# An audio tower on one core: row scales in two parts, the first batch normalised and projected between the last two convolution groups, and an earlier place for VectorE's shared-expert outputs

## The reference

```python
h = layernorm(conv(x, kernel 2, stride 2) + bias + pair_mean(x)) * gamma + beta   # 188 rows per batch
n = layernorm(h)
q, k, v = n@W_q, n@W_k, n@W_v
lat = (k + v) @ W_down_kv
o = softmax(q @ (lat@W_up_k).T / sqrt(256) * exp(-0.01*|t-s|)) @ (lat@W_up_v)     # 16 heads of 16
h = h + o @ W_o
n = layernorm(h)
h = h + experts(n) + (gelu(n@Sg.T) * (n@Su.T)) @ Sd.T   # 16 experts; each takes its 752 best tokens
```

## Time and profile before

| what | us |
|---|---|
| median of 3 runs (lowest, highest) | 1759.16 (1757.37, 1760.4) |
| the profiled execution: its time, its span in the trace | 1760.71, 1758.9 |
| TensorE, VectorE busy | 1628.6, 1211.9 |
| GpSimd, ScalarE busy | 1026.2, 933.0 |

### The profile page before, as it was taken

One profiled execution on the slowest core, in us unless ns is written; L12 is line 12 of the kernel. 1 busy time (PEld: TensorE's weight loads), 2 busy tenths in 40 slices (PEclk: granted clock), 3 DMA queues, 4 the chain that ended last, 5 costly groups with the idle time before them and its releaser, 6 DMA issues.

```text
span 1758.9 us, 46442 instructions
## 1 busy us (share of the span) xinstructions
PE 1628.6 (93%) x14944; PEld 1200.7 (68%) x14944; DVE 1211.9 (69%) x3836; ACT 933.0 (53%) x2182; POOL 1026.2 (58%) x1101
## 2 busy tenths in 40 slices
PE   5893899999999997899996899999999999999997
PEld 5882667777777774666664577777777777777775
DVE  3884889999999998757788555555555555555541
ACT  3543777777777775453345444444445544444431
POOL 3782265666666655732255446666776666666665
PEclk9995999999999999899998899999999999999999
DMA  6541455666666662432321323444433333434322
GB/s 187 161 141 36 116 146 134 152 151 153 145 145 150 150 150 78 140 79 69 96 79 58 144 81 89 105 106 106 108 102 102 102 90 98 104 85 104 83 32 29
DMA packets 181154, 192.95 MB, mean 110 GB/s; under 512 B 120776, under 2 KB 153928, under 8 KB 175176
## 3 DMA queue, kind: packets, MB, share of 16 engines
q1 hardware_dynamic: 145992, 141.19, 28.4%
q0 software_dynamic: 35072, 50.62, 14.1%
HBM read 134.59 MB, written 50.44 MB: 105 GB/s over the span
## 4 chain that ended last, share of the span: by engine, by line
PE 51%; DVE 3%; ACT 2%; issue 2%; POOL 1%; DMA 1%; SPq 1%; DVEq 0%; POOLq 0%; ACTq 0%
PE psum L1907 28%; PE psum L1926 14%; PE psum L1756 4%; PE psum L1773 2%; PE psum L1887 1%; DVE arena L1347 1%; PE psum L1817 1%; DVE hidden L1350 1%; POOL arena L461 0%; ACT arena L851 0%; DMA weights_lo<-e_u 0%; DVE arena L1317 0%; ACT arena L1041 0%; PE psum L1746 0%; ACT hidden L851 0%
## 5 line engine op out<-in xcount | busy, mean ns | idle before, releaser
L1907 PE MATMUL psum<-arena,hidden 128*128 128x376 f16 x3072 | 493.9, 323 | 2.4 <-DVE arena L1516 1.5
L1907 PEld LDWEIGHTS psum<-arena,hidden 128*128 128x128 f16 x3072 | 300.8, 98 | 191.4 <-DVE arena L1516 2.7
L743 POOL TENSOR_TENSOR arena<-arena 128x376 f16<-128x376 f32 x256 | 250.8, 982 | 201.3 <-ACT arena L851 199.9
L851 ACT ACTIVATE arena<-arena 128x376 f16<-128x376 f32 (+11 forms) x636 | 288.1, 464 | 63.4 <-DVE arena L1436 53.5
L1094 ACT ACTIVATE arena<-psum 128x376 f32<-128x376 f32 x256 | 123.7, 483 | 342.0 <-PE psum L1907 342.0
L1250 DVE CUSTOM_DVE_ANT_0 arena<-psum,constants 128x188 f32<-128x188 f32 x768 | 237.6, 347 | 53.0 <-PE psum L1584 42.9
L851 ACT ACTIVATE arena<-psum 128x188 f32<-128x188 f32 (+7 forms) x457 | 176.0, 398 | 165.3 <-PE psum L1887 72.2
L1516 DVE SCALAR_TENSOR_TENSOR arena<-psum,arena 128x376 f32<-128x376 f32 x256 | 140.5, 549 | 178.4 <-ACT arena L1094 176.7
L1926 PE MATMUL psum<-hidden,arena 128*128 128x256 f16 (+1 forms) x2304 | 256.6, 272 | 0.0
L1926 PEld LDWEIGHTS psum<-hidden,arena 128*128 128x128 f16 (+1 forms) x2304 | 230.3, 103 | 21.4
L900 ACT ACTIVATE arena<-psum 128x376 f32<-128x376 f32 x384 | 184.2, 481 | 81.1 <-PE psum L1598 80.1
(11 more groups left out here) (168 smaller groups left out, 2783.2 us busy)
## 6 DMA issues: line engine op xcount, KB each, us to landing
arena<-e_d SPq DMA_DIRECT2D x16, 1024.0 KB
arena<-e_g SPq DMA_DIRECT2D x15, 1024.0 KB
arena<-e_u SPq DMA_DIRECT2D x15, 1024.0 KB, 5.0
arena<-x_t SPq DMA_DIRECT2D x32, 376.0 KB, 3.4
weighed<-arena POOLq DMA_DIRECT2D x32, 376.0 KB, 3.7
arena<-q_halves SPq DMA_DIRECT2D x192, 47.0 KB, 3.1
arena<-k_halves SPq DMA_DIRECT2D x96, 94.0 KB, 2.3
arena<-q_halves SPq DMA_DIRECT2D x96, 94.0 KB, 2.2
```

The source lines that it names most:

```text
L743: nc.gpsimd.tensor_tensor(dst, f, hi, ALU.subtract).then_inc(ready, 1)
L851: return nc.scalar.activation(dst, src, ACT.Copy, scale=scale)
L1907: last = mm(bank[2 * (s % 2) + i][:, 0:CHUNK], w_, a, start=n == 0, stop=n == 5)
```

## The change

1. No engine meets between convolution and attention. The row scales come in two parts: tiles 0 to 47 (`NORMALS`) once `of_normal(11)` is done, on VectorE behind `of_conv(14)`; tiles 48 to 63 at the end, on ScalarE behind its body(-3).
2. Batch 0 is normalised, transposed and split between groups 14 and 15 (`before_last`), and its x, Q and K go to banks 0, 1 and 2, which group 14 has left. The buffers XN, XTH and XTL get places that the convolution stage doesn't use. TensorE waits, ahead of these transposes, for VectorE's gamma step of group 14 (batch 0) and 15 (batch 1).
3. In a step of the shared expert VectorE does `down_out` right after its product (L1436), ahead of `decide` and `count`. After the last step it does `down_out(43)` and `down_out(44)` ahead of the last four hot parts; before it was `down_out(43)` alone.
4. SP waits for `hot_quarter(2)` ahead of `load(0, 2)` and for `hot_quarter(3)` ahead of expert 1's weights.

```diff
@@ places
-        XN = at2(2 * D)
-        XTH, XTL = ([at2(2 * S, F16) for _ in range(2)] for _ in range(2))
+        at2.at += 2 * D + 4 * S
...
         V = [at2(3 * HP * 32) for _ in range(2)]
+        XN = at2(2 * D)
+        XTH, XTL = ([at2(2 * S, F16) for _ in range(2)] for _ in range(2))
@@ banks, and a hook in conv_groups (ScalarE, GpSimd)
+        def x_bank(c):
+            return bank[0] if isinstance(c, int) and c == 0 else XB
...
-            body(B // 2 - 2, 0, 3)
-            body(B // 2 - 1, 1, 3)
+            for g in range(2):
+                before_last(g)
+                body(B // 2 - 2 + g, g, 3)
@@ SP
             for i in range(OUTS):
                 sp.wait_ge(sh_out[i], outs_of(i))
+            sp.wait_ge(hot_used, 3)
             load(0, 2)
+            sp.wait_ge(hot_used, 4)
             sp.wait_ge(xg_in[0], 16 * SLOT_TILES)
@@ GpSimd
+            def before_last(g):
+                if g == 1:
+                    low_x(-3, 1)
@@ ScalarE (all five: - meet(...))
+            def scales(n, t0, t1):
+                act.wait_ge(rstd_done, 3 * n + 1)
+                nc.scalar.activation(SD[0:HT, t0:t1], MV[0:HT, t0:t1, 1], ACT.Sqrt, bias=C[0:HT, C_EPS:C_EPS + 1]).then_inc(sd2_done, 1)
...
+            def before_last(g):
+                if g == 0:
+                    scales(0, 0, NORMALS)
+                else:
+                    batch(-4, 0)
+                    batch(-3, 1, (0, 1))
+
+            conv_groups(act, conv_group, before_last)
+            batch(-3, 1, range(2, NS))
+            scales(1, NORMALS, TILES)
+            batches(act, batch, -2)
@@ VectorE
+            normals_done()
+            of_conv(B // 2 - 2, 0, 2)
+            scales(0, 0, NORMALS)
+            of_normal(B // 2 - 4)
+            of_conv(B // 2 - 1, 1, 2)
+            for g in range(B // 2 - 3, B // 2):
+                of_normal(g)
+            normals_done()
+            scales(1, NORMALS, TILES)
...
+                for j in downs_at(s - 1):
+                    down_out(j)
                 for b in row_batches(s, False)[:1]:
...
-                for j in downs_at(s - 1):
-                    down_out(j)
...
-                for j in downs_at(STEPS - 1):
+            for j in range(ST - 4, ST - 2):
                 down_out(j)
             for n in range(STEPS - HOT, 4 * E // QE):
                 hot_part(n)
             last_values()
-            for j in range(ST - 3, ST):
+            for j in range(ST - 2, ST):
                 down_out(j)
@@ TensorE, job
+                if n == 11 and isinstance(b, int) and b < -2:
+                    pe.wait_ge(lo_done, 4)
+                    pe.wait_ge(gam_done, 8 + CG * (B // 2 + 3 + b))
```

More of the change, by code:

```diff
@@ L322, in block_tile, with q_bank, k_bank, batches @@
             return blocks[:, a * CW + t * 128:a * CW + (t + 1) * 128]
-        def batches(eng, body):
-            for b in range(-4, 4):
+        def x_bank(c):
+            return bank[0] if isinstance(c, int) and c == 0 else XB
+        def q_bank(c):
+            return bank[1] if isinstance(c, int) and c == 0 else WB
+        def k_bank(c):
+            return bank[2] if isinstance(c, int) and c == 0 else WB
+        def batches(eng, body, first=-4):
+            for b in range(first, 4):
                 body(b, b % 2)
@@ L332, in batches, with conv_groups @@
                 body(b, b % 2)
-        def conv_groups(eng, body):
+        NORMALS = CG * (B // 2 - 4)
+        def conv_groups(eng, body, before_last):
             body(0, 0, 0)
@@ L524, in _ @@
                         sp.dma_start(v, value_rows if i == 6 else blank).then_inc(blanks_in, 16)
-            meet(sp)
             def read(blocks, dense, dram, c, single, par, landed):
@@ L673, in _ @@
                 low_input(j, j)
-            conv_groups(pool, conv_group)
-            meet(pool)
             def low(dst, src, hi, src_ready, c, ready):
@@ L729, in batch @@
                 spread_inverse(b - 1)
-            batches(pool, batch)
+            def before_last(g):
+                if g == 1:
+                    low_x(-3, 1)
+            conv_groups(pool, conv_group, before_last)
+            batches(pool, batch, -3)
             def low_first(p):
@@ L960, in keep_heads, with batch @@
                     copy(OS[cpar][:, g * S:(g + 1) * S], OB).then_inc(os_ready, 1)
-            def batch(b, par):
-                for n in range(NS):
+            def batch(b, par, steps=range(NS)):
+                for n in steps:
                     exponential(b, par, n)
                     if n == 0:
-                        evacuate(XF, XB, b + 3, xt_done, xf_ready)
+                        evacuate(XF, x_bank(b + 3), b + 3, xt_done, xf_ready)
                     elif n == 1:
@@ L994, in batch @@
                         evacuate_values(b + 2, 0)
-            batches(act, batch)
+            def before_last(g):
+                if g == 0:
+                    scales(0, 0, NORMALS)
+                else:
+                    batch(-4, 0)
[4 more added lines that the diff above has]
+            batches(act, batch, -2)
             def deviations(t0, t1):
@@ L1180, in _ @@
             conv_group(1, 1, 1)
-            with dve.Fori(0, B // 4 - 1) as i:
+            with dve.Fori(0, B // 4 - 2) as i:
                 conv_chain.enter(i, 4 * CG)
@@ L1185, in _, with normals_done, scales @@
                 conv_group(2 * i + 3, 1, 2)
-            conv_chain.leave(B // 4 - 1)
-            ln_chain.leave(B // 4 - 1)
-            for g in (B // 2 - 2, B // 2 - 1):
-                of_normal(g)
-            ln_chain.wait()
-            dve.sem_inc(rstd_done, 1)
-            dve.wait_ge(sd2_done, 1)
-            nc.vector.reciprocal(RSTD[0:HT, :, 0], SD[0:HT, :]).then_inc(rstd_done, 1)
-            dve.wait_ge(rstd_done, 2)
-            nc.vector.scalar_tensor_tensor(MSCALED[0:HT, :, 0], MV[0:HT, :, 0], -1.0, RSTD[0:HT, :, 0], ALU.mult, ALU.mult).then_inc(rstd_done, 1)
-            meet(dve)
+            conv_chain.leave(B // 4 - 2)
+            ln_chain.leave(B // 4 - 2)
+            def normals_done():
+                ln_chain.wait()
+                dve.sem_inc(rstd_done, 1)
+            def scales(n, t0, t1):
+                dve.wait_ge(sd2_done, n + 1)
+                nc.vector.reciprocal(RSTD[0:HT, t0:t1, 0], SD[0:HT, t0:t1]).then_inc(rstd_done, 1)
+                dve.wait_ge(rstd_done, 3 * n + 2)
+                nc.vector.scalar_tensor_tensor(MSCALED[0:HT, t0:t1, 0], MV[0:HT, t0:t1, 0], -1.0, RSTD[0:HT, t0:t1, 0],
+                                               ALU.mult, ALU.mult).then_inc(rstd_done, 1)
+            normals_done()
[4 more added lines that the diff above has]
+            for g in range(B // 2 - 3, B // 2):
+                of_normal(g)
+            normals_done()
+            scales(1, NORMALS, TILES)
             for par in range(2):
@@ L1573, in _ @@
                             last.then_inc(conv_done, 1)
-            meet(pe)
             def scores(b, par, n):
@@ L1631, in weigh, with project @@
                 last.then_inc(weighed, 1)
-            def project(c, par, w0, done):
+            def project(c, par, w0, done, to):
                 for g in range(2):
@@ L1639, in project @@
                         for w_, a in split3(WH[:, w], WL[:, w], XTH[par][:, x], XTL[par][:, x]):
-                            last = mm(WB[:, g * S:(g + 1) * S], w_, a, start=n == 0, stop=n == 5)
+                            last = mm(to[:, g * S:(g + 1) * S], w_, a, start=n == 0, stop=n == 5)
                             n += 1
```

20 lines of the change are left out of this document (10 added, 10 removed).

## The result

The changed kernel took **1747.63 us** (median of 4 runs, 1746.71 to 1748.59) against 1759.43 for the kernel before (4 runs, 1757.37 to 1760.4): ratio 0.9937, 95% interval 0.9925 to 0.9949, or 11.8 us faster by the medians and 9.0 to 13.2 by the interval. The prediction was 1737, so 22.8 us were expected and about half came. The time lies outside the range of 1730.5 to 1745. The two profiled executions differ by 13.7 (1760.71 and 1746.98), but they are one run each.

A forecast was written before the change was run, and what follows sets the result against it. TensorE, busy 93% of the span, was taken as the bound, its idle time as the possible gain. Head 13.0, middle 2.5 and end 7.3 sum to 22.8 us, giving 1737 us, range 1730.5 to 1745.

The forecast's parts named there:

- Head: Convolution to attention: batch 0's early work and scales in two parts shorten TensorE's idle, 13.0 us, bounds 11.0 to 14.0.
- The bound named for ScalarE's cover: Head: gain falls to 11.0 us if ScalarE's three operations ahead of group 15 overrun their 1.2 us cover by 2 us.
- Middle: Shared expert's steps: `down_out` ahead of the search removes TensorE's 7 waits of 4.6 us in sum; 2.5 us won.
- Between 0 and 4.6 I take **2.5: Middle's bounds: up to 4.55 us may return as waits for `count` inside GpSimd's subtraction, but not each time.
- the 5 that the prediction itself named as a sign of being wrong: Shared expert's steps: TensorE's waits for `count` above 5 us would show the prediction wrong; 1 to 3 us were expected.
- The slower rival: Shared expert: the search becomes the bound, 1.08 us on each of about 22 steps, giving 1762.7 us; 2 in 100.
- End: End of the shared expert: earlier `down_out(44)` lets token transposes start at 970.8, not 978.14; 7.3 us, bounds 3.3 to 9.3.
- The gathers' 970.8: End: all six gathers are in at 970.41 plus 0.43, so the token transposes start at 970.8.
- the load that the prediction let hide behind expert 0's matmuls: End: `load(0, 2)` has until expert 0's third step and hides behind its matmuls.
- SP's two new waits help here: End: with SP's waits on the hot quarters, expert 1's weights no longer run beside quarter 3.
- Sum: Whole kernel: 13.0 + 2.5 + 7.3 = 22.8 us faster; 20.5 to 24 us had 50 in 100.
- The first rival, code fetching: Last hot quarters: code fetching holds them, so the end wins 3.3 and the sum 18.8 us, 1740.5 us; 18 in 100.

The follow-up runs named there:

- e6: The changed kernel with the old place of `down_out` in the steps and the old end, so only the head is changed: 1745.32 us, ratio 0.9921.
- e1: The changed kernel with `down_out` behind `decide` and `count` in every step, as before the change: 1743.86 us, ratio 0.9917.
- e2: The changed kernel with `down_out` early only from step 18, in its old place before that: 1741.72 us, ratio 0.9871.
- e3: The changed kernel with SP's score writes, GpSimd's use of them and the token table's writes 8 steps later: 1740.17 us, ratio 0.9871.
- b2: The kernel before with the changed end of the shared expert alone: 1756.13 us against 1756.39, ratio 1.0.
- b1: The kernel before, unchanged, profiled a second time: 1760.87 us, one run.
- e7: The changed kernel with the old end of the shared expert alone: 1748.84 us, ratio 0.9941.
- e10: The changed kernel with GpSimd's six gathers for expert 0 held back until the last hot quarter is done: 1750.04 us, one run.
- e9: The changed kernel with score writes and their first use 8 steps later, and `load(0, 2)` behind SP's wait for the gathers: 1734.96 us, ratio 0.9885.
- e4: The changed kernel with `load(0, 2)` behind SP's wait for the gathers: 1746.89 us, ratio 0.9907.
- e5: The changed kernel with one more small matmul between the last hot quarter and the token transposes: 1746.6 us, one run.

## Why the prediction was wrong

**Head: right, term and steps.** 13.0 was predicted, 13.4 measured at the first scores and 13.9 (11.3 to 16.5 by the interval) as a time (e6). `x_norm(0)` at 134.0 (133.70), group 12's copy to 136.4 (136.24), Q's write at 145.3 (145.17), XF(1) at 149.3 (148.95), scores at 156.2 (156.09). The bound named for ScalarE's cover was never touched.

**Middle: this step failed.** The gain was right: 2.5 predicted and 2.8 measured from step 19 to 50. It comes as the text had it: 4.6 us of waits of `down` gone, 1.9 of waits for `count` back. That the two numbers are so near is in part luck, for 2.5 was a choice between 0 and 4.6, made on the ground that the collision would not be met each time, and it is met in 21 of 27 counts. What failed is the bound "Between 0 and 4.6 I take **2.5**". The text costed `down_out` ahead of `decide` and `count` at its 0.43 us, and listed GpSimd's subtraction as the only thing that could hold the search. It did not ask what else `down_out` itself waits for. Its residual comes from SP, whose queue has the eight writes of the token table just then, and the row that shows it was in the trace of before: `down_out` waited 1.36 us at 788.04 with "DMA arena<-hidden" behind it. Behind `count` that wait was harmless; ahead of it, the next sum, and so TensorE, waits too. That is 6.3 us at step 15, shown by e1, e2 and e3, each of which removes it. With it the waits for `count` are 7.4 us in sum (760 to 890 us), above the 5 that the prediction itself named as a sign of being wrong. The part of it that is lost at the lower clock was in no term. The windows of the earlier trace rows began at 790, just behind the place. The slower rival had the right queue, but with 1.08 us on each of 22 steps rather than one long wait.

**End: the term was mis-sized, 7.3 against nothing that can be measured.** (0 with 1.6 us of error in b2, 1.5 and 1.8 inside the error on another chip.) Two causes, both shown in the traces; what the second is worth as a time is not resolved.
- *The baseline was one execution.* The quarters' 13.3 us were 7.9 in the second trace of the same code (b1), and 7.9 again in e6 and e7. The move could save only what lay above that. The text saw that this idle had no semaphore behind it, and treated its coming back as a loss on the changed kernel. It did not consider that the kernel before might usually not have it.
- *The next wait moved.* "The gathers' 970.8" was taken as fixed and as the new bound, 23.1 us after step 63. By b1's 25.2 that still leaves 2.1. The last quarter came where it was predicted: 964.8 to 968.2 there, and 955.91 + 8.9 = 964.8 to 968.1 here, the 8.9 being what the trace is ahead at step 63. The transposes, by the same count, came at 973.3 instead of 970.8. But the load that the prediction let hide behind expert 0's matmuls now goes up in the middle of the gathers, and the transposes start 6.5 us after the last issue rather than 2.9 (e10) or 3.0 (e9). The end stays at 25.6.

"SP's two new waits help here" was wrong as well: the wait on the third quarter was long over when SP reached it, for SP was waiting for the output tiles, and the other came after the load that did the harm.

**Sum.** 13.4 - 6.3 + 2.8 + 0 = 9.9 us, inside the measured 9.0 to 13.2. The remaining 1.9 to the median is of the size by which the attention stage varies, and no cause is claimed for it. The profiled pair's 13.7 counts otherwise, 4.9 for the end, because it starts from the first trace with its long end. The first rival, code fetching, gave 1740.5, nearer but 7 us early, and by the wrong route: the idle it was built on was in the kernel before, and in the changed kernel's trace both quarters ran in one piece.

## What to carry to other kernels

Before an instruction is put ahead of others in an in-order queue, list every input that it waits for anywhere in the trace, not only the one that is wanted early. A wait of 1.4 us that nobody noticed behind the search cost 6.3 ahead of it. Idle time that no semaphore explains may belong to one execution: profile the unchanged kernel a second time before counting on it. And when a late step is pulled forward, look at what the other queues may then start sooner; here it was a 1 MB load in the middle of the gathers that were the next bound.

## What the runs showed of the hardware

- TensorE's idle under "issue" inside straight runs of small matmuls comes and goes: two quarters took 13.3 and 7.9 us in two traces of the same program, and the last quarter 3.2 to 3.3 us in some executions and 7.3 to 7.8 in others (e2, e3, e4, e5). The Trainium skill (Runtime: NRT & Kernel Launch, "Instruction fetch mechanics") says that code is fetched while the engine runs and that this is mostly hidden. If it is fetching, these traces show it unhidden by 1.4 to 6 us at this place; no run here shows that it is.
- An indirect gather on GpSimd took 6.35 us beside VectorE's 56 table instructions, until their end, and 1.11 without them.
- TensorE's granted clock fell from 1.00 to 0.50 within a wait of 5.58 us at step 15, and was back at 1.00 some 4.7 us after the work went on. The 1.47 us wait of the kernel before left it at 1.00.
- VectorE's tensor_tensor of one column took 158 to 161 ns by itself or when it started ahead of GpSimd's subtraction, and up to 815 when it started inside one, ending with it (21 of 27 in the changed kernel, 9 of 27 before).
- SP's first load that waits for the six gathers went up 3.0 to 4.0 us after the last gather's issue (six traces), and 6.2 to 6.9 with a 1 MB load issued 0.1 to 1.1 us ahead of that gather (five traces).
